# Self attention of a decoder block: product of multiplier and score with its maximum in one VectorE operation a batch

## The reference, cut to what matters

```python
qkv = x @ W_qkv + b_qkv;  q, k, v = split(qkv)
attn = einsum('bsd,btd->bst', q, k) * SCALE
# sps_pro: each score is multiplied by a number that depends on its own size
xn = sigmoid(attn)
mult = where(xn > .95, 2.0, where(xn > .85, 1.5, where(xn < .1, 0.1, where(xn < .25, 0.3, 1.0))))
attn = softmax(attn * mult, axis=-1)
out = einsum('bst,btd->bsd', attn, v) @ W_proj + b_proj
x = layernorm(x + out)
```

## Time and profile before

| | |
|---|---|
| median of three runs | 1502.25 us (1501.21 to 1502.8) |
| profiled execution, its own time | 1503.4 us |
| its span, first to last instruction | 1501.6 us |
| busy: TensorE / VectorE / GpSimd / ScalarE | 92% / 80% / 78% / 58% of the span |
| `attention` stage | some 13 to 152 us of the span |

### The profile page before, as it was taken

The page is one execution under the profiler, slowest core; times in us unless marked ns, Lnnn a source line. Parts: engine busy times, 40 slices in busy tenths (PEclk is TensorE's granted clock), DMA queues, the critical chain, the costliest instruction groups (busy, mean ns, idle before and its releaser), DMA issues. The chain is left out here.

```text
span 1501.6 us, 34958 instructions
## 1 busy us (share of the span) xinstructions
PE 1378.7 (92%) x12862; PEld 1098.9 (73%) x12862; DVE 1199.1 (80%) x2383; ACT 873.7 (58%) x1542; POOL 1164.6 (78%) x1032
## 2 busy tenths in 40 slices
PE   5765599999999977999999999995999999999998
PEld 4654366666666655777777777764999999999998
DVE  4998466677666765888888888876899999999996
ACT  2677244454454434777777677762666666656665
POOL 5443466666666644999999999993899999999997
PEclk9898599999999998999999999998999999999999
DMA  5110243333333305222222222211232232232231
GB/s 162 37 36 13 84 126 103 92 93 104 108 96 93 91 19 169 78 78 77 78 78 80 81 78 77 78 64 57 75 90 78 87 96 81 78 96 81 79 96 29
DMA packets 77194, 123.81 MB, mean 82 GB/s; under 512 B 8353, under 2 KB 45794, under 8 KB 77026
## 3 DMA queue, kind: packets, MB, share of 16 engines
q1 hardware_dynamic: 75426, 117.16, 24.9%
q0 software_dynamic: 1088, 4.19, 1.0%
q10 hardware_dynamic: 512, 0.23, 0.1%
HBM read 70.28 MB, written 51.27 MB: 81 GB/s over the span
## 5 line engine op out<-in xcount | busy, mean ns | idle before, releaser
L942 POOL TENSOR_TENSOR gather_d<-gather_e,gather_rinv 128x1024 f32<-128x1024 f32 x128 | 244.9, 1913 | 46.2 <-DVE gather_rinv L921 46.2
L1176 PEld LDWEIGHTS mix_Y<-kept_phi,mix_cT 128*128 128x128 f32 x2048 | 248.3, 192 | 7.2
L1257 POOL TENSOR_TENSOR mix_c<-mix_e,mix_rinv 128x1024 f32<-128x1024 f32 x128 | 240.9, 1903 | 16.0 <-DVE mix_rinv L1217 13.8
L1176 PE MATMUL mix_Y<-kept_phi,mix_cT 128*128 128x128 f32 x2048 | 249.1, 275 | 0.0
L1192 ACT COPY mix_cT<-mix_T 128x1024 f32<-128x1024 f32 x128 | 128.5, 1004 | 135.6 <-PE mix_T L1183 135.6
L1214 DVE TENSOR_REDUCE mix_sums<-mix_e 128x16 f32<-128x1024 f32 x128 | 155.7, 1217 | 32.0 <-ACT mix_e L1197 31.6
L917 DVE TENSOR_REDUCE gather_rsum<-gather_e 128x32 f32<-128x1024 f32 x128 | 156.1, 1220 | 26.2 <-ACT gather_e L890 26.2
L773 POOL TENSOR_TENSOR cross_kd<-cross_pack,kept_consts 128x624 fp32r<-128x624 f32 x128 | 155.4, 1234 | 24.5 <-DMA cross_pack<-cross_halves 24.1
L936 POOL TENSOR_TENSOR gather_dl<-gather_d,gather_dh 128x512 fp32r<-128x512 f32 x128 | 166.1, 1298 | 0.0
L618 ACT ACTIVATE cross_pT<-cross_P 77x1024 f32<-77x1024 f32 x128 | 130.5, 1022 | 49.5 <-PE cross_P L545 49.5
L879 ACT COPY gather_keep<-gather_L 128x256 f32<-128x256 f32 x256 | 94.8, 370 | 104.6 <-PE gather_L L853 97.3
(11 more groups left out here) (189 smaller groups left out, 3177.5 us busy)
## 6 DMA issues: line engine op xcount, KB each, us to landing
kept_logits<-gather_keep SPq DMA_DIRECT2D x128, 256.0 KB, 2.0
mix_read<-kept_logits SPq DMA_DIRECT2D x64, 512.0 KB, 3.7
cross_halves<-cross_qk SPq DMA_DIRECT2D x32, 412.0 KB, 3.3
cross_pack<-cross_halves SPq DMA_DIRECT2D x64, 128.0 KB
cross_pack<-cross_halves SPq DMA_DIRECT2D x32, 206.0 KB
cross_pack<-cross_halves SPq DMA_DIRECT2D x64, 78.0 KB
attn_xTg<-in_xT SPq DMA_DIRECT2D x16, 256.0 KB, 2.7
kept_xres<-in_x POOLq DMA_DIRECT2D x4, 1024.0 KB, 12.4
```

What stands on the lines that cost most here:

```text
L942: pool.tensor_tensor(dd[u % 4][:].rearrange("p i (n s) -> p i n s", n=16), e[u % 2][:], rinv[u % 2][:].rearrange("p (i n) -> p i n", i=2). ...
L1176: ins = pe.matmul(psY[t % 2][:, 0:128], cT[u % 2][:, c, :], w.yk[:, 8 * (u % 2) + c, :], start=(u % 2 == 0 and c == 0), stop=(u % 2 == 1 a ...
L1257: pool.tensor_tensor(cc[u % 2][:], e[u % 2][:], rinv[u % 2][:].unsqueeze(2).to_broadcast([128, 16, EXPERTS]), ALU.mult)\
```

## The change

The two VectorE operations on the 128x512 tile, product and maximum, are replaced by four operations, one for each batch of 128x128. Each writes the product of its batch to `f2` and, with its accumulator that starts at -FILL, the maximum of the product to one column of `mx`. The wait on `f2_done` between the two old operations is gone with them. The last of the four raises `mx_done`. On VectorE's list each of the four is two instructions: the product (128x128, out of `band[5]` and `a`) and a read of the accumulator (128x1, to `mx`), so that eight stand where two stood, all with line number L375. Lines behind it are one higher: L380 is L381, L384 is L385. Nothing else differs, on VectorE or on another engine.

```diff
-                    dve.tensor_tensor(f2[g % 2][:], band[5][:], av, ALU.mult).then_inc(f2_done, 1)
-                    dve.wait_ge(f2_done, g + 1)
-                    dve.tensor_reduce(mx[:], f2[g % 2][:].rearrange("p (b t) -> p b t", b=GB), X, ALU.max)\
-                       .then_inc(mx_done, 1)
+                    for b in range(GB):
+                        c = slice(b * 128, (b + 1) * 128)
+                        ins = dve.tensor_tensor_reduce(f2[g % 2][:, c], band[5][:, c], av[:, c], 1.0, -FILL, ALU.mult, ALU.max,
+                                                       accum_out=mx[:, b:b + 1])
+                    ins.then_inc(mx_done, 1)
```

## The result

| | before | changed |
|---|---|---|
| median | 1501.97 us (1501.12 to 1505.04, 6 runs) | 1493.97 us (1493.54 to 1494.86, 6 runs) |
| ratio | | 0.9946, 95% interval 0.9936 to 0.9956 |
| profiled execution, its span | 1503.4 us, 1501.6 us | 1493.79 us, 1491.9 us |
| barrier behind `attention`, next stage's first operation on VectorE | 156.49 us | 147.36 us |

Faster by 8.0 us where 1.6 were forecast, and outside the range of 1497.0 to 1508.0. Two further measurements of the same kernel on other chips gave 0.9948 (0.9937 to 0.996) and 0.9953 (0.994 to 0.9967), that is 7.9 and 7.4 us less.

The account below looks back on a forecast made before the run. VectorE's list was taken to bound the attention stage. 4 x 0.23 + 3 x 0.07 + 0.18 = 1.31 us against 1.44 saves 0.13 in 13 groups, 1.7 us: 1500.6 us against 1502.25, range 1497.0 to 1508.0.

Parts of the forecast that it names:

- VectorE's list is the bound of the stage: Attention stage, 45 to 150 us: VectorE works without a gap, 7.52 us a step, so its savings ahead of L384 count.
- Product, p = 0.23 us: Distance between starts of the four 128x128 products, taken as the middle between 0.197 and 0.262 us.
- Read, r = 0.07 us: Each accumulator read on VectorE adds 0.07 us, as between two 128x1 results; ScalarE's read gave 0.09.
- outer bound: A product's 128 columns alone at 0.137 us: 0.94 us a group, with the saving stopped at 0.46 by GpSimd.
- Tail 0.18 us: From the last read's start to L385: one 128x1 duration of 0.15 us and a hand-over of 0.03.
- Count of 13 groups: Of 16 groups a saving counts in 13, being swallowed behind groups 0, 1 and 3; a loss counts 14 times.
- The cover behind groups 1 and 3: L334 starts right on TensorE's V behind group 1 and waits 0.53 us for TensorE behind group 3, swallowing savings.
- GpSimd's room, saving capped at 0.46: GpSimd's L223 ends 0.49 us before L380 starts, the narrowest room; a group's saving stops at 0.46 us.
- L223 would not be stretched: GpSimd's L223, 1.46 us beside VectorE, was costed at nothing extra; stretched by 0.6, some 0.2 us a group lost.
- Rival A: The eight VectorE instructions don't overlap: 1.75 us a group, a loss of 0.31, 1506.6 us; chance 0.17.
- Rival B: Each product with an accumulator runs at half rate: net 0.42 us lost a group, 1508.1 us; chance 0.08.
- Rival C: Products 0.197 and reads 0.07 us or less: saving 0.26 or more a group, 1498.9 us, 1496.3 at best; chance 0.25.

Follow-up runs that it names:

- the memset of 580 columns: Changed kernel with a useless 128x580 memset on VectorE ahead of the masks in every group: 1502.91 us, 1.0002 of the kernel before.
- early groups: Changed kernel with fused operations only in groups 0 to 3, the old product and maximum in groups 4 to 15: 1501.65 us, 0.9996 of the kernel before.
- late shift: Changed kernel with the layer norm's shift moved from before `nb` to behind the next step's masks: 1496.81 us, 0.9957 of the kernel before.
- 64 columns: Changed kernel with eight fused operations of 64 columns for four of 128, `nb` from half of each batch: 1499.67 us, 0.998 of the kernel before.

## Why the prediction was wrong

- *VectorE's list is the bound of the stage*: right. The step fell from 7.52 to 7.05 us, all of it VectorE's, and the memset of 580 columns took it back.
- *Product, p = 0.23 us*: 0.213. The bounds of 0.197 and 0.262 held it. 4 x 0.017 = 0.07 us a group.
- *Read, r = 0.07 us*: this step failed. I priced the read as one more 128x1 operation in the row, by a copy and by ScalarE's read. On VectorE it starts with the next product and moves the one behind it by 0.01 us, which the 0.213 above already holds: 3 x 0.07 = 0.21 us a group too much. My outer bound was made for the product alone; for the read I named two rows and took the lower as the end, with zero left out.
- *Tail 0.18 us*: 0.11. The read lasts 0.08 us, not the 0.15 of a 128x1 copy. 0.07 us a group. The three sum up to 0.35: 1.31 forecast, 0.97 measured, just outside the 0.98 to 1.86 us beyond which I had said I would be wrong.
- *Count of 13 groups*: 15 in an execution with full clock. The cover behind groups 1 and 3 in the earlier trace rows belongs to single executions, and I took it for a property of the kernel. Four profiles of kernels with fused operations have it (no reads, early groups, late shift, 64 columns: waits of 0.15 to 0.33 us behind group 1, in two of them 0.93 and 1.12 behind group 3), at a mean granted clock of 0.61 to 0.78 from 33 to 36 us; the three of the changed kernel, at 0.96 to 1.00 there, don't. Group 0's is in every profile.
- *GpSimd's room, saving capped at 0.46*: right in place and size. The saving came to 0.47, with L381 0.04 us behind L223, and the next 0.25 us were stopped by it. That VectorE's own block had shrunk to just this length is luck: I had reached the cap only with an outer bound on the product and the read at 0.07. *L223 would not be stretched*: right, 1.46 us as before.
- *Rival A, paid in full durations*: wrong. Fused products of 0.28 us start 0.213 us apart, plain ones of 0.29 us 0.20 us, and the block is 0.97 us, not 1.75. I had drawn on the Trainium skill, page "VectorE: DVE Perf Modes", section "The DRAIN you can't avoid", for it, and left out the sentence of that section by which a next operation that isn't held back starts earlier. These starts agree with that sentence, and paying eight full durations was my reading, not the page's.
- *Rival B, half rate*: wrong, 692 ns for 512 columns with an accumulator, as without. The sentence of the page "Vector Engine (DVE) Microarchitecture Reference", section "Points that are easy to get wrong", of the Trainium skill is on `S2S2D2_STT`; the trace lists the fused operation as a custom one, and no run shows whether the sentence is meant for it. What the runs show is that it doesn't hold for this operation.
- *Rival C, better overlap*: right in kind, at a quarter of the chance. Its typical size, 3.4 us, was too small for the reason named at the read, and its best, 1496.3 us, still lay above the measured time, by the count and by the unsettled rest below.

From forecast to result: the price of a group gives 13 x (0.474 - 0.13) = 4.5 us more than the 1.7 forecast, the two further groups 0.9, together 15 x 0.474 = 7.1 us of the 7.4 to 8.0 measured. The rest, 0.3 to 0.9 us, is not settled. Two things work in its direction, and neither is shown to come from the change. One is the earlier load of x, 0.3 to 1.3 us between profiles. The other is TensorE's granted clock: two of four profiles of the kernel before had falls in the early steps, with waits of up to 1.8 us at L334, none of three of the changed one, but the kernel without reads had such falls at a step of 7.03 us.

## What to carry to other kernels

A chain of fused operations on VectorE that don't wait for each other costs the distance of their starts, some 0.08 us and 1.06 ns a column here with the reads in it, and a read of the accumulator adds 0.01 us to it; so fusing two passes paid off here even though it cut one tile into four. Bound each new instruction below by zero if the trace has no row of that very kind. Before a wait is counted as cover, look whether the granted clock of that stretch is one that every execution has. And before a difference of two profiles is credited to a change, look for what already differs ahead of the first changed instruction.

## What the runs showed of the hardware that I had not expected

- The read of VectorE's accumulator starts at the same time as the next product, at 64 and at 128 columns, and lasts 0.08 us. At 128 columns products are 0.213 us apart with it and 0.205 without.
- A fused product and maximum with two float32 sources in SBUF runs at the rate of the plain product (692 ns on 512 columns).
- A step longer by 0.2 us (7.73 for 7.52) can cost over twice its price (8.2 us at the median for 3.4): in the execution of 1516.1 us TensorE's granted clock fell again and again in the same stage, and steps of 9.35 us alternated with those of 7.72. At 7.88 us, with a memset in another place, the profile has only two such waits behind the first, of about 0.5 us.
- A mask on GpSimd of 128x512 took 1.93 us where VectorE needs 0.34 from start to start.
